# B laid out once per unit, and one VectorE product instruction over both groups, in a four-layer selective-scan kernel

## The reference

```
dts, B, C = split(x_dbl)                  # projections of the convolved input u
delta = softplus(dts @ W_dt + bias)
for l in positions:                       # per image, channel d and state n
    h = exp(delta[l] * A) * h + (delta[l] * u[l]) * B[l]
    y[l] = sum over n of h * C[l]
```

## Time and profile before

| what | value |
|---|---|
| median of 3 runs | 36397.42 us (36394.28 to 36398.0) |
| span of the profiled execution, first to last instruction | 36378.3 us |
| what lies around the span, against the median | 19.1 us |
| DVE busy over the span | 33161.5 us (91%) |
| POOL busy | 30847.6 us (85%) |
| PE busy, modelled | 26866.7 us (74%) |
| ACT busy | 18959.8 us (52%) |
| mean granted TensorE clock | 0.848 of full speed |

### The profile page before, as it was taken

How to read it: one execution, slowest core, us unless ns; L and a number is a source line. 1 busy time by engine, 2 the same in 40 slices (tenths; PEclk the granted TensorE clock), 3 DMA queues, 4 the chain that set the end, 5 groups by cost and what they waited for, 6 DMA issues and landing times. The chain is left out here.

```text
span 36378.3 us, 340417 instructions
## 1 busy us (share of the span) xinstructions
PE 26866.7 (74%) x79280; PEld 8195.4 (23%) x79280; DVE 33161.5 (91%) x18001; ACT 18959.8 (52%) x23286; POOL 30847.6 (85%) x7804
## 2 busy tenths in 40 slices
PE   5777777777766777777777766777777777766777
PEld 2222222222222222222222222222222222222224
DVE  5999999999977999999999977999999999976993
ACT  4555555555534555555555534555555555534551
POOL 1999999999961999999999951999999999964994
PEclk7888888888888888888888888888888888887886
DMA  4666666666675666666666665666666666675665
GB/s 154 173 172 174 175 173 175 174 173 174 173 221 168 175 172 174 175 174 175 174 174 174 174 216 168 174 174 173 173 175 175 174 174 174 174 218 181 175 174 148
DMA packets 2423694, 6402.41 MB, mean 176 GB/s; under 512 B 703824, under 2 KB 875728, under 8 KB 2411728
## 3 DMA queue, kind: packets, MB, share of 16 engines
q1 hardware_dynamic: 2421968, 6387.69, 65.8%
HBM read 2986.75 MB, written 764.47 MB: 103 GB/s over the span
## 5 line engine op out<-in xcount | busy, mean ns | idle before, releaser
L1277 POOL TENSOR_TENSOR h<-h,c 128x2048 f32<-128x2048 f32 x4992 | 20780.7, 4179 | 660.1 <-DVE h L1077 522.6
L1077 DVE TENSOR_TENSOR_SCAN h<-decay,state,slot 128x1024 f32<-128x1024 f32 x6240 | 14647.7, 2347 | 789.0 <-ACT state L1221 32.3
L906 PE MATMUL slot<-bc,pick 96*128 96x512 bf16 x12496 | 4544.6, 452 | 7554.3 <-DVE h L1073 6883.1
L983 PE MATMUL psy<-h,t_fold 128*32 128x512 f32 x40000 | 9979.5, 671 | 0.0
L1073 DVE TENSOR_TENSOR_SCAN h<-slot,state,made 128x1024 f32<-128x1024 f32 x3744 | 8548.9, 2325 | 6.5 <-ACT slot L1116 5.3
L1298 POOL TENSOR_TENSOR made<-du,b 128x2048 f32<-128x2048 f32 x1872 | 7811.8, 4173 | 683.0 <-DMA b<-bcdram 683.0
L1116 ACT ACTIVATE decay<-delta,na 128x1024 f32<-128x1024 f32 x6248 | 7102.1, 1146 | 1892.8 <-DVE h L1077 1701.4
L1051 DVE TENSOR_TENSOR slot<-du,slot 128x1024 f32<-128x1024 f32 x6240 | 7540.3, 1208 | 374.1 <-PE slot L906 342.9
L1116 ACT ACTIVATE slot<-delta,na 128x1024 f32<-128x1024 f32 x3744 | 4181.7, 1117 | 4061.1 <-DVE h L1077 4046.9
L906 PEld LDWEIGHTS slot<-bc,pick 96*128 96x128 bf16 x12496 | 841.0, 103 | 12915.3 <-DVE h L1073 9747.3
L983 PEld LDWEIGHTS psy<-h,t_fold 128*32 128x32 f32 x40000 | 2098.1, 119 | 7316.1 <-issue 7055.7
(11 more groups left out here) (111 smaller groups left out, 19571.9 us busy)
## 6 DMA issues: line engine op xcount, KB each, us to landing
delta<-delta SPq DMA_DIRECT2D x10048, 128.0 KB, 2.5
du<-du SPq DMA_DIRECT2D x10048, 128.0 KB, 2.9
b<-bcdram SPq DMA_DIRECT2D x7520, 128.0 KB, 2.8
c<-bcdram SPq DMA_DIRECT2D x6720, 128.0 KB, 2.9
u<-useq SPq DMA_DIRECT2D x212, 1536.0 KB, 6.7
yseq<-ybuf SPq DMA_DIRECT2D x624, 512.0 KB, 2.8
ya<-yseq SPq DMA_DIRECT2D x420, 512.0 KB, 4.8
yb<-yseq SPq DMA_DIRECT2D x360, 512.0 KB, 5.8
```

Of the source, the lines that this page charges most:

```text
L906: mm = pe.matmul(slot[s % 2][:, cols], pick[:, rows_of, :], bc[q % 2][:, cols], start=True, stop=True)
L983: mm = pe.matmul(psy[rows, cols], T["fold"][:, :], h[v % H_RING][:, c, cols], start=(v % QUADS == 0), stop=(v % QUADS == QUADS - 1), skip_ ...
L1077: dve.tensor_tensor_scan(out, decay[s % DECAY_RING][:, order], slot[s % 2][:, order], first, ALU.mult, ALU.add).then_inc(sem["h_ready"], 1)
L1277: pool.tensor_tensor(both[:, :, 0:CH], both[:, :, 1:], c4[g][:, order].unsqueeze(1).broadcast_to((P, 2, CH)), ALU.mult)\
```

## The change

TensorE fills only `slot[0]`, once for each vector unit. One VectorE instruction of 2 x 1024 elements a partition makes both products: it reads `slot[0]` twice (a broadcast over the group dimension) and walks the groups backward, so that group 1's product goes into `slot[1]` first and group 0's then goes over B itself in `slot[0]`. The two slots become one PSUM tensor `slots`. Since the instruction writes `slot[1]`, which the scan just before it may still read, it waits for that scan's `h_ready`. DVE's order in a unit goes from product, scan, product, scan to product, scan, scan. The counts of `b_full` go by units, and the product adds 2 to `b_multiplied`.

```diff
+    def filled(v):
+        return v + 1 - sum(w <= v for w in on_pool)
...
-        slot = [ctx.enter_context(nc.psum_tensor(f"slot{j}" + W["tag"], [P, CH], F32)) for j in range(2)]
+        slots = ctx.enter_context(nc.psum_tensor("slots" + W["tag"], [P, 2, CH], F32))
+        slot = [slots[:, j, :] for j in range(2)]
...
-                def fill_b(C0, s, first=False):
+                def fill_b(C0, v, first=False):
-                    body, s = s // BS, s % BS
-                    q, t, n = place(s)
-                    if s // 2 in on_pool:
+                    body, v = v // BU, v % BU
+                    q = v // UNITS
+                    if v in on_pool:
                         return
-                    S = (C0 + body * BODY_CHUNKS) * STEPS + s
+                    S = (C0 + body * BODY_CHUNKS) * STEPS + 2 * v
...
                     if not first:
                         pe.wait_ge(sem["h_ready"], S + (H_START - 1))
...
-                        mm = pe.matmul(slot[s % 2][:, cols], pick[:, rows_of, :], bc[q % 2][:, cols],
+                        mm = pe.matmul(slot[0][:, cols], pick[:, rows_of, :], bc[q % 2][:, cols],
...
                     for s in range(BS):
-                        fill_b(C0, s + FILL_LAG)
+                        if s % 2 == 0:
+                            fill_b(C0, s // 2 + 1)
...
-                def multiply(C0, body, s):
-                    q, t, n = place(s)
-                    count = by_vector(s)
-                    dve.wait_ge(sem["b_full"], body * by_vector(BS - 1) + count)
-                    j = pair_of(s // 2)
-                    if s // 2 % QUADS == 0 or s // 2 % QUADS == 1 and s // 2 - 1 in on_pool and s % 2 == 0:
+                def multiply(C0, body, v):
+                    dve.wait_ge(sem["b_full"], body * filled(BU - 1) + filled(v))
+                    dve.wait_ge(sem["h_ready"], C0 * STEPS + (2 * v + H_START))
+                    j = pair_of(v)
+                    if v % QUADS == 0 or v % QUADS == 1 and v - 1 in on_pool:
                         dve.wait_ge(du_in[j % DU_RING], body * DU_BODY + du_count(j))
-                    dve.tensor_tensor(slot[s % 2][:], du4[j % DU_RING][:, s % 2, 1:], slot[s % 2][:], ALU.mult)\
-                        .then_inc(sem["b_multiplied"], 1)
+                    dve.tensor_tensor(slots[:, ::-1, :], du4[j % DU_RING][:, ::-1, 1:],
+                                      slots[:, 0:1, :].broadcast_to((P, 2, CH)), ALU.mult)\
+                        .then_inc(sem["b_multiplied"], 2)
...
-                        for s in range(BS):
-                            q, t, n = place(s)
-                            if s // 2 not in on_pool:
-                                multiply(C0, body, s)
-                            scan(C0, body, s, g)
+                        for v in range(BU):
+                            if v not in on_pool:
+                                multiply(C0, body, v)
+                            scan(C0, body, 2 * v, g)
+                            scan(C0, body, 2 * v + 1, g)
```

More of the change, by code:

```diff
@@ L61 @@
 H_RING, DECAY_RING, DELTA_RING, DU_RING, B_RING, MADE_RING = 4, 3, 3, 2, 2, 2
-AHEAD, FILL_LAG, REDUCE_LAG = 2, 2, 2
+AHEAD, REDUCE_LAG = 2, 2
 FLAT = 2 * NS * CH // P
@@ L891, in _ @@
             def _(pe):
-                def fill_b(C0, s, first=False):
-                    body, s = s // BS, s % BS
-                    q, t, n = place(s)
-                    if s // 2 in on_pool:
+                def fill_b(C0, v, first=False):
+                    body, v = v // BU, v % BU
+                    q = v // UNITS
+                    if v in on_pool:
                         return
-                    S = (C0 + body * BODY_CHUNKS) * STEPS + s
-                    if t == 0 and n == 0:
+                    S = (C0 + body * BODY_CHUNKS) * STEPS + 2 * v
+                    if v % UNITS == 0:
                         pe.wait_ge(sem["bc_in"], (C0 + body * BODY_CHUNKS) * 16 + 16 * (q + 1))
@@ L903, in fill_b @@
                         pe.wait_ge(sem["h_ready"], S + (H_START - 1))
-                    rows_of = batch_of(s // 2) * QUADS + s // 2 % QUADS
+                    rows_of = batch_of(v) * QUADS + v % QUADS
                     for cols in HALF:
-                        mm = pe.matmul(slot[s % 2][:, cols], pick[:, rows_of, :], bc[q % 2][:, cols],
+                        mm = pe.matmul(slot[0][:, cols], pick[:, rows_of, :], bc[q % 2][:, cols],
                                        start=True, stop=True)
@@ L1005, in _ @@
                 pe.wait_ge(sem["pick_in"], 16)
-                for s in range(FILL_LAG):
-                    fill_b(0, s, first=True)
+                fill_b(0, 0, first=True)
                 with pe.Fori(0, NC // BODY_CHUNKS) as i:
@@ L1114, in decay_of @@
                         act.wait_ge(sem["h_ready"], S + (H_START - DECAY_RING + 1))
-                        dst = decay[s % DECAY_RING]
-                    act.activation(dst[:], delta4[j % DELTA_RING][:, s % 2, :], ACT.Exp, scale=na[q][:, k:k + 1])\
+                        dst = decay[s % DECAY_RING][:]
+                    act.activation(dst, delta4[j % DELTA_RING][:, s % 2, :], ACT.Exp, scale=na[q][:, k:k + 1])\
                         .then_inc(sem["decay_ready"], 1)
```

## The result

The changed kernel takes 35932.64 us (median of 4 runs, 35923.16 to 35936.29) against 36397.71 before: a ratio of 0.9873 (95% interval 0.9861 to 0.9885), 465 us or 1.28% faster. Forecast were 36,295, which is 102 us faster, and a range from 36,090 to 36,500.

What follows compares the result with a forecast made beforehand. DVE was taken as the bound, POOL 1.6 us a tile behind. Terms of -119 (DVE's tile sum), -45 (PE) and +62 (ACT) made -102 us: a span of 36276, with 19 us around it 36,295; range 36,090 to 36,500.

Steps and rivals of the forecast that it cites:

- Product to scan becomes 1.36 + 1.07 = 2.43 us: On DVE, start of fused product to its scan: 1.36 us for 1024 elements, plus 1.07 for 1024 more.
- So an own wait costs 0.08 + 0.12: On DVE, waiting for its own last instruction loses 0.08 us of overlap and 0.12 of gap, 0.20 in all.
- now handled in the open: Before products of two units in eight, a satisfied du_in wait behind the blocking one: 0.02 us taken, 0 to 0.12 possible.
- The sum over a tile: DVE's products and scans in a tile: 49.29 us before, 49.13 after; 0.19 taken as gained, 119 us over 624 tiles.
- the ACT term: ACT's second decay at unit 2 of a tile comes 0.1 us late for DVE, once a tile: +62 us.
- The product's duration: The fused product on DVE, 2 x 1024 elements, was to have a mean near 2.28 to 2.30 us.
- The wait on the scan: On DVE, scan start to the start of a product that waits for it: 2.325 + 0.12 = 2.44 us.
- Rival 1: DVE's own wait is free, saving 1.0 us a tile more until POOL binds: 35,650 to 36,090, say 35,900; chance 0.06.
- -45 forecast: DVE's waits for PE's late fills in the scan stages: half of some 92 us gone, -45 us.
- rival 4: Slower: fills and decays miss the shorter window, PE's clock falling after idle; 36,480 to 36,610, at worst 36,900; chance 0.13.
- The 19 us around the span: Time added outside the kernel's own span: 36276 us plus 19 gave the forecast of 36,295.

Runs made afterwards that it cites:

- e14: Changed kernel with the fill adding 2 to b_full, so product and scan wait for the same number again: 36154.7 us, 0.9936.
- e1: Changed kernel, B still laid out once, but two products of 1024 elements instead of the fused one: 35926.18 us, 0.9871.
- e2: Kernel before, with each of the 6240 products also waiting for the scan just in front (h_ready): 37259.47 us, 1.0237.
- e4: Changed kernel, with the second scan of each vector unit also waiting for the first (h_ready): 36289.92 us, 0.997.
- e8: Changed kernel with each fill written twice, four matmuls instead of two, same values: 36137.68 us, 0.9928.
- e7: Changed kernel with ACT's copy of the next chunk's first projection at step 14 of tile 0 instead of 12: 35885.74 us, 0.9858.
- e3: Kernel before, with the scan's waits for decay_ready, reduced and state_saved moved in front of its step's product: 36050.85 us, 0.9905.
- e13: Kernel before, with the product adding 2 instead of 1 to b_multiplied and the scan waiting for twice the count: 36052.79 us, 0.9909.
- e6: Changed kernel, with the product's wait for du_in put ahead of the one for h_ready: 35907.46 us, 0.9866.

## Why the prediction was right or wrong, point by point

**The step that failed** is "Product to scan becomes 1.36 + 1.07 = 2.43 us", and under it "So an own wait costs 0.08 + 0.12". I read the gap of 0.10 to 0.13 behind the product as the wait's own latency, and carried it over to the new scans. It is 0.035 of latency, and a further 0.07 to 0.10 because the wait for the product stood on an EVENT_SEMAPHORE in front of the scan. The very effect that I priced for `du_in` ("now handled in the open") was in the old scan's rows already. In the changed kernel one scan in two has no product in front any more, as I had counted, but at the others the gap fell to 0.035: product to scan is 2.33 measured. At 3120 products 0.10 us is 311 us of DVE's time. Put back by e14 it costs 222 us, of the 363 that the forecast missed.

**The sum over a tile was right for the program that I had in mind.** The changed kernel with equal counts (e14) shows 2.43 from product to scan, 7.12 for a unit (7.13 summed) and 4.67 behind POOL units (4.68). It takes 36,155, 140 us under the forecast of 36,295. Of these, 59 are the ACT term, which was hardly lost there (38.0 us of waits for the decay, 34.7 before, where +62 was counted), and 21 are waits for PE, which are 66 us below before, not 45. Another 43 are the tile of the kernel before: by the starts of its scans the median tile took 49.38 us, where I summed 49.29, against 49.12 in e14, where I summed 49.13. That is 0.26 a tile gained instead of 0.19. The last 17 or so are open.

**The product's duration:** 2.28 to 2.30 forecast, 2.297 measured. But the fusion as built is worth nothing (e1): the 0.06 that it saves it gives back at its start, since it adds 2.

**The wait on the scan:** 2.44 forecast from scan to product, 2.43 to 2.44 measured, and this is luck: the price of 0.20 came from a gap with an EVENT_SEMAPHORE in it, and the new product happens to have one too. With the wait on the instruction itself it is 0.14 to 0.15 (e2, e4). The rule of the Trainium skill ("VectorE: DVE Perf Modes", "The DRAIN you can't avoid"), by which a semaphore between VectorE instructions costs nothing extra, does not hold here: 867 us for 6240 waits. Rival 1 named about the measured time, 35,900, by a mechanism that is refuted; that the number was near is no merit of it.

**PE:** -45 forecast, -44 measured (342.9 to 298.6), with the clock lower as said (0.829 against 0.848). The double fill (e8) shows that the window is tight: rival 4's shortage is real, but it needs twice the fills.

**ACT:** +62 forecast at unit 2's second decay; +71 measured (5.3 + 29.4 to 106.1), but at unit 7 of tile 0, behind a copy that waits for PE (e7). The size was luck, the place wrong.

**The 19 us around the span:** there are 1.7. The profiled execution after took 35929.24 with a span of 35927.5. The rest of the 19 is that before's profiled execution lay some 17 us below the median of its runs. The forecast is the median less 102 all the same, so this shifted nothing.

**POOL:** it is busy for 97% of the stretch in the scan stage, and it waits for DVE's scans 238.8 us in all, 658.8 before. That leaves little room for a further gain on DVE alone.

Like with like, the change itself is worth 120 us where the scan's blocking wait stands on the scan in both kernels (36,053 to 35,933), and 244 where it stands in front in both (36,399 to 36,155); each of these differences is known to some 60 to 75 us. The rest of the 465 us came from where the wait landed, which a register instruction decided.

## What to carry to other kernels

Before pricing a wait from a gap, look in the trace at which instruction the blocking wait stands on. It should be the computing instruction itself, with all waits that are long satisfied on earlier ones. Here that was worth 341 to 346 us (0.95%) with no change to the work, by moving waits up (e3) or by a count that needs its own register instruction (e13). A product that added 2 to its semaphore never had its wait on itself, which cost it 0.07 us. And when a restructured kernel gains, run the parts alone: merging the instruction gained nothing here, while an accident of counting gained about half of the 465 us or more (221 to 345). The 120 to 244 us of the layout go with the halved fills, as waits for PE are 298.6 us against 492.4 in e13; that these waits are the cause is argued and not shown by a run of its own.

## What the hardware showed that I had not expected

- A VectorE instruction that waits for the one in front starts 0.035 us behind its recorded end when the wait stands on itself (after, e1, e2, e4, e13). It starts 0.09 to 0.105 behind when the wait stands on an EVENT_SEMAPHORE in front (before, after, e2, and at all 3120 products of e6), and 0.133 when that one also holds a second wait behind the blocking one, though this is long satisfied (before, e14).
- Behind a blocking wait on a register instruction, with an EVENT_SEMAPHORE in between, it is 0.19 (after); 0.12 with the satisfied wait on the product itself (e1).
- An own wait costs 0.14 to 0.15 us if it stands on the instruction (e2, e4): 0.08 of overlap, 0.035 of gap and some 0.02 in the record of the instruction itself.
- The length of the product, 1024 or 2048 elements, changes neither start.
